# Softmax attention on one Trainium2 core: all four quarters of the value product directly behind the sums

## Chip, cores, metric

One NeuronCore of a Trainium2 chip runs the whole program. The metric is the device time of one execution in microseconds (us), taken as the median of several runs. The program has nine stages one after the other; the change touches only the softmax attention.

## What is computed

The program is a small network on x of shape (8, 512, 128): a quantised feed-forward layer, softmax attention, the feed-forward layer again, a mixture of experts, six layers of linear attention, the mixture again. The attention has 16 heads of 64, computed on the layer norm of x and added to x:

```python
q = split_heads(x @ Wq.T); k = split_heads(x @ Wk.T); v = split_heads(x @ Wv.T)
sim = jnp.einsum('bhid,bhjd->bhij', q, k) * scale
attn = safe_softmax(sim)
out = jnp.einsum('bhij,bhjd->bhid', attn, v)
return out.transpose(0, 2, 1, 3).reshape(B, N, INNER) @ Wo.T + bo
```

## The kernel before

The attention (attn_stage, L544 to L873) works on pairs of heads. A unit g is one pair of one batch, so there are 8 x 8 = 64 units (0 to 63), each with 512 queries and 512 keys. Every engine has its own hand-written loop over periods g = -2 to 66, and the engines meet through semaphores. In period g, TensorE (PE) works on several units at once: the scores of g+1, the transposed scores of g, the value product of g-1, the output product of g-3 and the projections of g+2. A period has four parts, kt = 0 to 3, one for each quarter of 128 keys (or of 128 queries):

- scores_turned(g, kt), L760 to L770: three pairs of fp16 products (high and low halves of q and k) write the transposed scores of a quarter of the keys into the banks turned[0] and turned[1], one for each head. The pair of one step runs on different row halves of the array. Each head's first product waits until ScalarE (ACT) has taken the exponential of the quarter before out of that head's bank (exp_done). less_maximum(g, kt), L772 to L778, is the fourth pair: it subtracts the row maxima, and its end lets ACT go (exp, L707 to L713).
- scores(g+1, qt), L742 to L750: a pair of fp16 products for a quarter of the queries of the next unit, written to score[0] and score[1]. It waits until VectorE (DVE) has reduced the quarter before (s_read). neg_max, L620 to L626, is that pair of DVE reductions. I call the products of part kt "turned kt" and "scores kt".
- project(g+2, 0) in part 0 and project(g+2, 1) in part 2, L780 to L799: the projections of q and of k, three fp16 products each. They go to the one bank proj. ACT copies the high half out (high, L694) and DVE then forms the low half (low, L636 to L642). project(g, 2) in part 3, L800 to L805, is the projection of v, twelve products into the same bank, and so it waits for low of k of unit g+2 (lo_done).
- max_turned(g+1), L752 to L758, at the end of part 3: one product that transposes the maxima. It waits for all eight reductions of unit g+1 (s_read at 8(g+2)). DVE turns its result into mdiag (max_rows, L628), which less_maximum of part 0 of the next period needs.
- add_up(g-1), L807 to L817, in part 1: the sums of the exponentials, from the tiles that GpSimd (POOL) adds up on L611. Behind it ACT (total_out), DVE (invert, L648) and eight SBUF copies on SyncE's queue (L596) prepare the reciprocals with which DVE normalises a period later (L655, o_done).
- values(g-1, kt), L819 to L828: a quarter of the value product, one fp32 product for each head (on different column halves of the array), accumulated in the bank pv over the four quarters. The first quarter waits for o_done of the unit before. The last quarter's end is pv_done, which lets ACT overwrite v and the exponentials two units on.
- output(g-3), L830 to L839: four fp32 products in part 0.

PE's order inside a period is only that of the code at L842 to L872. The value product stands in three places of it: quarters 0 and 1 in part 1, quarter 2 behind project(g+2, 1), quarter 3 in front of project(g, 2).

Of the kernel before, what the change touches and what calls it, by code (L numbers as in the profile page):

```python
# [18 lines left out]
TPB = 4  # L19
# [524 lines left out]
def attn_stage(nc, mem, tag):  # L544
# [5 lines left out]
    with ExitStack() as ctx:  # L550
# [29 lines left out]
        live = lambda g: 0 <= g < PAIRS_ALL  # L580
        PERIODS = range(-2, PAIRS_ALL + 3)

        with nc.Block() as block:
# [155 lines left out]
            def _(pe):  # L739
                XY = [(0, 0), (0, 1), (1, 0)]  # L740

                def scores(g, qt):  # L742
                    if qt == 0:
                        pe.wait_ge(hi_done, 2 * g + 2)
                    if g or qt:
                        pe.wait_ge(s_read, 8 * g + 2 * qt)
                    for head in range(2):
                        rows = halves[head]
                        nc.tensor.matmul(score[head][:], high_of[0][g % RING][rows, qt * P:(qt + 1) * P], high_of[1][g % RING][rows, :],  # L749
                                         start=True, stop=True).then_inc(s_done, 1)  # L750

                def max_turned(g):  # L752
                    pe.wait_ge(s_read, 8 * (g + 1))
                    if g:
                        pe.wait_ge(m_out, g)
                    if g >= 2:
                        pe.wait_ge(total_done, g - 1)
                    nc.tensor.transpose(max_bank, nmax[:], mem["ident"][:]).then_inc(m_done, 1)  # L758

                def scores_turned(g, kt):  # L760
                    k = g % RING
                    tile = slice(kt * P, (kt + 1) * P)
                    if kt == 0:
                        pe.wait_ge(lo_done, 2 * g + 2)
                    for n, (k_of, q_of) in enumerate(((high_of, high_of), (high_of, low_of), (low_of, high_of))):
                        for head in range(2):
                            if n == 0 and (g or kt):
                                pe.wait_ge(exp_done, 8 * g + 2 * kt + head - 1)
                            rows = halves[head]
                            nc.tensor.matmul(turned[head][:], k_of[1][k][rows, tile], q_of[0][k][rows, :], start=(n == 0), stop=False)  # L770

                def less_maximum(g, kt):  # L772
                    if kt == 0:
                        pe.wait_ge(m_out, g + 1)
                    for head in range(2):
                        rows = halves[head]
                        nc.tensor.matmul(turned[head][:], unit[rows, :], mdiag[rows, :, :].rearrange("p t q -> p (t q)"), start=False,  # L777
                                         stop=True).then_inc(t_done, 1)  # L778

                def project(g, which):  # L780
                    b, pair = divmod(g, PAIRS)
                    cols = slice(pair * P, (pair + 1) * P)
                    w = mem["w_attn16"][:, which]
                    x = lambda part_i, first, n: mem["xT"][:, part_i, b * SEQ + first:b * SEQ + first + n]
                    if which == 0:
                        if g >= 3:
                            pe.wait_ge(v_out, g - 2)
                        if g:
                            pe.wait_ge(lo_done, 2 * g)
                    elif which == 1:  # L790
                        pe.wait_ge(lo_done, 2 * g + 1)
                    else:
                        pe.wait_ge(lo_done, 2 * min(g + 3, PAIRS_ALL))
                        if g:
                            pe.wait_ge(v_out, g)
                    if which < 2:
                        for i, (w_part, x_part) in enumerate(XY):
                            last = nc.tensor.matmul(proj[:], w[:, w_part, cols], x(x_part, 0, SEQ), start=(i == 0), stop=(i == 2))  # L798
                        last.then_inc(qk_done, 1)  # L799
                    else:  # L800
                        for t in range(TPB):
                            for i, (x_part, w_part) in enumerate(XY):
                                last = nc.tensor.matmul(proj[:, t * P:(t + 1) * P], x(x_part, t * P, P), w[:, w_part, cols],
                                                        start=(i == 0), stop=(i == 2))
                        last.then_inc(v_done, 1)  # L805

                def add_up(g):  # L807
                    pe.wait_ge(added, 2 * (g + 1))
                    if g:
                        pe.wait_ge(total_done, g)  # L810
                    pe.wait_ge(m_out, min(g + 2, PAIRS_ALL))
                    for head in range(2):
                        for half in range(2):
                            first = (2 * head + half) * QUAD
                            last = nc.tensor.matmul(sums[first:first + QUAD, 0:HALF], ones[:],
                                                    psum[g % 2][:, head, half * HALF:(half + 1) * HALF], start=True, stop=True)
                    last.then_inc(sums_done, 1)  # L817

                def values(g, kt):  # L819
                    if kt == 0:  # L820
                        pe.wait_ge(v_out, g + 1)
                        if g:
                            pe.wait_ge(o_done, g)
                    for head in range(2):
                        last = nc.tensor.matmul(pv[halves[head], :], vv[g % 2][:, kt, halves[head]], pT[g % 2][:, head, kt, :],  # L825
                                                start=(kt == 0), stop=(kt == TPB - 1))
                    if kt == TPB - 1:
                        last.then_inc(pv_done, 1)  # L828

                def output(g):  # L830
                    pair = g % PAIRS
                    pe.wait_ge(o_done, g + 1)
                    if pair == 0 and g:
                        pe.wait_ge(x_added, g // PAIRS)
                    for t in range(TPB):
                        tile = slice(t * P, (t + 1) * P)
                        last = nc.tensor.matmul(out[:, tile], oT[g % 2][:, tile], mem["woT"][:, pair, :],
                                                start=(pair == 0 and t == 0), stop=(pair == PAIRS - 1), skip_group_check=True)
                    last.then_inc(out_done, 1)  # L839

                pe.wait_ge(set_up, 2)
                for g in PERIODS:  # L842
                    for kt in range(TPB):
                        if live(g):
                            scores_turned(g, kt)
                            if kt:
                                less_maximum(g, kt)
                        if live(g + 1):
                            scores(g + 1, kt)
                        if kt == 0:  # L850
                            if live(g):
                                less_maximum(g, 0)
                            if live(g + 2):
                                project(g + 2, 0)
                            if live(g - 3):
                                output(g - 3)
                        elif kt == 1 and live(g - 1):
                            add_up(g - 1)
                            values(g - 1, 0)
                            values(g - 1, 1)  # L860
                        elif kt == 2:
                            if live(g + 2):
                                project(g + 2, 1)
                            if live(g - 1):
                                values(g - 1, 2)
                        elif kt == 3:
                            if live(g - 1):
                                values(g - 1, 3)
                            if live(g):
                                project(g, 2)  # L870
                            if live(g + 1):
                                max_turned(g + 1)  # L872
# [765 lines left out]
```

## Time and profile before

| | |
|---|---|
| median of 3 runs | 2076.28 us (2074.09 to 2078.01) |
| profiled execution | 2078.86 us, span 2077.1 us |
| PE, DVE, ACT, POOL busy over the span | 74%, 71%, 42%, 49% |
| attention (first to last product on PE) | about 254 to 1071 us |
| PE, DVE, ACT, POOL busy between 400 and 600 us | 200.00, 152.27, 99.33, 122.60 us |
| granted PE clock between 400 and 600 us | 1.00 |

The span is the time from the first to the last recorded instruction; the execution's own time is 1.8 us longer. Matmul records overlap (the next one starts before the modelled end of the one before), so the time that a group of products takes on PE is read from the start of the group to the start of what follows it, not from its busy time.

### The profile page before, as it was taken

To read this page: it belongs to the slowest core of one execution; us is meant where nothing else is said; L and a number is where in the kernel's file an instruction comes from. 1 tells how busy PE (TensorE), PEld (TensorE's weight loads), DVE (VectorE), ACT (ScalarE), POOL (GpSimd) and SP (SyncE) were. 2 spreads that over 40 slices of the span, in tenths; PEclk is the share of its full clock that TensorE was granted. 3 is DMA by queue.
4 is the path that set the end of the run, shared out by engine and by line. 5 is a ranking of instruction groups with operands and counts; after the bars stand their busy time and mean duration, and the time that the engine had idled before them with its cause. 6 is when DMAs were issued, how large, how long until landed. Compare 5 with 4: busy or idle time off the path is not lost. (4 is left out here: it accounts for less than half of the span.)

```text
span 2077.1 us, 32008 instructions
## 1 busy us (share of the span) xinstructions
PE 1545.9 (74%) x10355; PEld 871.5 (42%) x10355; DVE 1483.7 (71%) x3141; ACT 865.7 (42%) x2102; POOL 1021.2 (49%) x1332
## 2 busy tenths in 40 slices
PE   0556389999999999999965554249748888761596
PEld 0334233334333333333323444227437767651373
DVE  4888677777777777777758887438567777773484
ACT  0111345444544445454422222037336667630372
POOL 0111346666565666565632222747435555627473
PEclk9889689999999999999986886569879999975698
DMA  6000000000000000000000000223400000002235
GB/s 199 0 0 1 1 11 23 23 23 22 21 21 22 24 23 22 22 21 21 24 19 0 1 0 6 72 70 108 126 1 1 1 1 1 1 11 72 75 109 156
DMA packets 90179, 70.51 MB, mean 34 GB/s; under 512 B 16608, under 2 KB 84640, under 8 KB 90016
## 3 DMA queue, kind: packets, MB, share of 16 engines
q1 hardware_dynamic: 75776, 44.05, 7.9%
q0 software_dynamic: 8704, 18.89, 2.7%
q10 hardware_dynamic: 5536, 5.52, 0.9%
q8 instruction: 87, 1.43, 0.3%
q14 instruction: 76, 0.62, 0.1%
HBM read 29.32 MB, written 22.30 MB: 25 GB/s over the span
## 5 line engine op out<-in xcount | busy, mean ns | idle before, releaser
L625 DVE TENSOR_REDUCE at_nmax<-at_score 128x1 f32<-128x512 f32 x512 | 329.9, 686 | 143.3 <-PE at_score L749 143.3
L713 ACT ACTIVATE at_pT<-at_turned 128x512 f32<-128x512 f32 x512 | 277.9, 595 | 342.8 <-PE at_turned L777 342.8
L611 POOL TENSOR_TENSOR m_rows<-m_rows,at_pT 128x512 f32<-128x512 f32 x256 | 319.5, 1269 | 95.0 <-ACT at_pT L713 95.0
L611 POOL TENSOR_TENSOR m_rows<-at_pT 128x512 f32<-128x512 f32 x128 | 160.2, 1271 | 227.6 <-ACT at_pT L713 227.6
L825 PE MATMUL at_pv<-at_pT,at_v 128*64 128x512 f32 x1024 | 261.7, 611 | 0.3 <-DVE at_oT L655 0.3
L1016 POOL DMA_INDIRECT by_token<-m_ysb,m_dest x144 | 137.9, 957 | 88.3 <-DVE m_ysb L1096 54.1
L1010 POOL DMA_INDIRECT by_expert<-m_rows,m_slot x128 | 123.5, 965 | 73.5 <-issue 38.4
L419 PE MATMUL f_gate<-m_wguT,f_xqT 128*128 128x352 f32 x128 | 63.3, 583 | 104.2 <-DVEq L337 102.8
L365 POOL TENSOR_TENSOR f_hq<-f_hg,f_hsc 128x704 f32<-128x704 f32 x32 | 44.3, 1384 | 195.2 <-DVEq L341 195.2
L115 DVE TENSOR_SCALAR la_xn<-la_y,la_ln_mean,la_ln_rstd 128x128 f32<-128x128 f32 x192 | 81.5, 485 | 53.6 <-POOLq L1438 53.6
L381 ACT ACTIVATE f_silu<-f_gate 128x704 f32<-128x704 f32 x32 | 24.2, 757 | 220.5 <-PE f_up L420 220.5
L648 DVE RECIPROCAL m_rows<-m_rows 128x256 f32<-128x256 f32 x64 | 111.6, 1743 | 2.9 <-ACT m_rows L719 2.9
L798 PE MATMUL at_proj<-m_rows 128*128 128x512 f16 x384 | 108.4, 392 | 5.3 <-DVE at_own L669 3.6
L1267 PE MATMUL m_h<-m_w,m_x 128*128 x432 | 109.8, 392 | 3.0 <-DVE m_x L1073 3.0
L1256 PE MATMUL m_x<-m_ident,m_xin 128*128 128x128 f32 x144 | 23.8, 292 | 112.8 <-DMA m_xin<-by_expert 112.8
L825 PEld LDWEIGHTS at_pv<-at_pT,at_v 128*64 128x64 f32 x1024 | 56.8, 135 | 117.6 <-issue 117.6
L770 PE MATMUL at_turned<-at_high_q,at_high_k 64*128 64x512 f16 x512 | 102.2, 388 | 0.8 <-ACT at_pT L713 0.5
L749 PE MATMUL at_score<-at_high_k,at_high_q 64*128 64x512 f16 x512 | 99.3, 381 | 2.8 <-DVE at_nmax L625 2.1
L770 PE MATMUL at_turned<-at_low_q,at_high_k 64*128 64x512 f16 x512 | 98.9, 378 | 0.0
L777 PE MATMUL at_turned<-at_mdiag,at_unit 64*128 64x512 f16 x512 | 98.8, 378 | 0.0
L770 PE MATMUL at_turned<-at_high_q,at_low_k 64*128 64x512 f16 x512 | 98.8, 377 | 0.0
L1500 PE MATMUL la_th<-m_ident,la_xn 128*128 128x128 f32 x192 | 33.8, 302 | 70.2 <-DVE la_xn L115 68.2
(311 smaller groups left out, 3665.4 us busy)
## 6 DMA issues: line engine op xcount, KB each, us to landing
m_rows<-m_rows SPq DMA_DIRECT2D x512, 32.0 KB, 1.8
m_xin<-by_expert SPq DMA_DIRECT2D x144, 72.0 KB
m_rows<-by_token SPq DMA_DIRECT2D x32, 256.0 KB, 4.8
by_token<-m_ysb,m_dest POOLq DMA_INDIRECT x144, 2.4
m_x<-in_x SPq DMA_DIRECT2D x8, 256.0 KB, 4.9
by_expert<-m_rows,m_slot POOLq DMA_INDIRECT x128, 2.3
out_x<-m_x SPq DMA_DIRECT2D x8, 256.0 KB, 3.9
by_expert<-m_pad SPq DMA_DIRECT2D x18, 72.0 KB, 1.6
```

The source lines that it names most:

```text
L611: done = nc.gpsimd.tensor_tensor(acc, before, pT[g % 2][:, head, kt, :], ALU.add)
L625: nc.vector.tensor_reduce(nmax[:, head * DH + qt:head * DH + qt + 1], score[head][:], AX.X, ALU.max, negate=True)\
L648: nc.vector.reciprocal(packed, total).then_inc(packed_done, 1)
L713: nc.scalar.activation(pT[g % 2][:, head, kt, :], turned[head][:], ACT.Exp).then_inc(exp_done, 1)
L749: nc.tensor.matmul(score[head][:], high_of[0][g % RING][rows, qt * P:(qt + 1) * P], high_of[1][g % RING][rows, :], start=True, stop=True). ...
L770: nc.tensor.matmul(turned[head][:], k_of[1][k][rows, tile], q_of[0][k][rows, :], start=(n == 0), stop=False)
L777: nc.tensor.matmul(turned[head][:], unit[rows, :], mdiag[rows, :, :].rearrange("p t q -> p (t q)"), start=False, stop=True).then_inc(t_don ...
L798: last = nc.tensor.matmul(proj[:], w[:, w_part, cols], x(x_part, 0, SEQ), start=(i == 0), stop=(i == 2))
L825: last = nc.tensor.matmul(pv[halves[head], :], vv[g % 2][:, kt, halves[head]], pT[g % 2][:, head, kt, :], start=(kt == 0), stop=(kt == TPB ...
L1010: nc.gpsimd.indirect_dma_start(dram_rows, bass.IndirectOffsetOnAxis(slot[:, k, t:t + 1], 0), rows[k][:, t, :], None).then_inc(scattered, 16)
L1016: nc.gpsimd.indirect_dma_start(mem["dram_y_all"], bass.IndirectOffsetOnAxis(dest[j // TPB % DESTS][:, j % TPB:j % TPB + 1], 0), ysb[q % YS ...
L1267: last = nc.tensor.matmul(h[j % 3][:], x16[n % 2][:, x_part, tile], mem["w12_16"][:, w_part, ds(e, 1), :].rearrange("p e h -> p (e h)"), s ...
```

## The change

PE's order inside a period changes. The quarters 2 and 3 of the value product, which stood behind the projection of k and in front of the projection of v, now follow quarters 0 and 1 directly in part 1. No instruction is added or removed, on any engine, and no wait is edited.

```diff
@@ -856,16 +856,11 @@
                                 output(g - 3)
                         elif kt == 1 and live(g - 1):
                             add_up(g - 1)
-                            values(g - 1, 0)
-                            values(g - 1, 1)
-                        elif kt == 2:
-                            if live(g + 2):
-                                project(g + 2, 1)
-                            if live(g - 1):
-                                values(g - 1, 2)
+                            for part in range(TPB):
+                                values(g - 1, part)
+                        elif kt == 2 and live(g + 2):
+                            project(g + 2, 1)
                         elif kt == 3:
-                            if live(g - 1):
-                                values(g - 1, 3)
                             if live(g):
                                 project(g, 2)
                             if live(g + 1):
```

PE's order from the sums in part 1 to turned 3, before (at_turned are the transposed scores, at_score the scores, at_proj a projection, at_pv the value product; L770 and L777 are the four pairs of scores_turned and less_maximum):

```order
L815 MATMUL at_sums<-m_rows 32x256 x4
L825 MATMUL at_pv<-at_pT,at_v 64x512 x4
L770 MATMUL at_turned<-at_high_q,at_high_k 128x512 x2
L770 MATMUL at_turned<-at_low_q,at_high_k 128x512 x2
L770 MATMUL at_turned<-at_high_q,at_low_k 128x512 x2
L777 MATMUL at_turned<-at_mdiag,at_unit 128x512 x2
L749 MATMUL at_score<-at_high_k,at_high_q 128x512 x2
L798 MATMUL at_proj<-m_rows 128x512 x3
L825 MATMUL at_pv<-at_pT,at_v 64x512 x2
```

The same place now:

```order
L815 MATMUL at_sums<-m_rows 32x256 x4
L825 MATMUL at_pv<-at_pT,at_v 64x512 x8
L770 MATMUL at_turned<-at_high_q,at_high_k 128x512 x2
L770 MATMUL at_turned<-at_low_q,at_high_k 128x512 x2
L770 MATMUL at_turned<-at_high_q,at_low_k 128x512 x2
L777 MATMUL at_turned<-at_mdiag,at_unit 128x512 x2
L749 MATMUL at_score<-at_high_k,at_high_q 128x512 x2
L798 MATMUL at_proj<-m_rows 128x512 x3
L770 MATMUL at_turned<-at_high_q,at_high_k 128x512 x2
```

Eight value products stand behind the sums where four stood, and turned 3 follows the projection of k directly.

PE's order from scores 3 to the next period, before, with the semaphores that each product waits for:

```order
L749 MATMUL at_score<-at_high_k,at_high_q 128x512 [waits at_s_read]
L749 MATMUL at_score<-at_high_k,at_high_q 128x512
L825 MATMUL at_pv<-at_pT,at_v 64x512 x2
L803 MATMUL at_proj<-m_rows 128x128 [waits at_v_out,at_lo_done]
L803 MATMUL at_proj<-m_rows 128x128 x11
L758 MATMUL at_sums<-m_ident,at_nmax 128x128 [waits at_total_done,at_m_out,at_s_read]
L770 MATMUL at_turned<-at_high_q,at_high_k 128x512 [waits at_exp_done,at_lo_done]
```

The same place now:

```order
L749 MATMUL at_score<-at_high_k,at_high_q 128x512 [waits at_s_read]
L749 MATMUL at_score<-at_high_k,at_high_q 128x512
L803 MATMUL at_proj<-m_rows 128x128 [waits at_v_out,at_lo_done]
L803 MATMUL at_proj<-m_rows 128x128 x11
L758 MATMUL at_sums<-m_ident,at_nmax 128x128 [waits at_total_done,at_m_out,at_s_read]
L770 MATMUL at_turned<-at_high_q,at_high_k 128x512 [waits at_exp_done,at_lo_done]
```

Between scores 3 and the transposition of the maxima only the projection of v is left.

## Rows read from the trace of the kernel before

**Rows 1.** Groups of instructions, PE, 281 to 1043 us: count | busy us, mean ns | idle before.

```profile
L825 PE MATMUL at_pv<-at_pT,at_v 128*64 128x512 f32 x976 | 249.9, 612 | 0.0
L758 PE MATMUL at_sums<-m_ident,at_nmax 128*128 128x128 f32 x61 | 17.0, 278 | 0.0
```

**Rows 2.** Line L758, all its instructions: duration ns min/median/max, first and last start.

```profile
L758 PE MATMUL at_sums<-m_ident,at_nmax x64: 277/278/474, 268.8 to 1052.3; 128*128 128x128 f32 x64
```

**Rows 3.** Timeline of a steady period: start us, duration us, engine, line [idle before].

```profile
608.59 1.94 PE L825 MATMUL at_pv<-at_pT,at_v 128*64 128x512 f32 x8
...
610.46 0.39 PE L770 MATMUL at_turned<-at_high_q,at_high_k 64*128 64x512 f16 x2
...
611.34 0.38 PE L749 MATMUL at_score<-at_high_k,at_high_q 64*128 64x512 f16 x2
611.53 1.09 ACT L713 ACTIVATE at_pT<-at_turned 128x512 f32<-128x512 f32 x2 [2.26 <-PE at_turned L777]
611.65 0.82 PE L798 MATMUL at_proj<-m_rows 128*128 128x512 f16 x3
611.75 1.29 DVE L625 TENSOR_REDUCE at_nmax<-at_score 128x1 f32<-128x512 f32 x2 [0.67 <-PE at_score L749]
...
612.40 1.08 PE L825 MATMUL at_pv<-at_pT,at_v 128*64 128x512 f32 x4
612.51 0.60 ACT L699 ACTIVATE at_high_k<-at_proj 128x512 f16<-128x512 f32 x1
613.14 0.69 DVE L641 SCALAR_TENSOR_TENSOR at_low_k<-at_proj,at_high_k 128x512 f16<-128x512 f32 x1
613.41 0.39 PE L770 MATMUL at_turned<-at_high_q,at_high_k 64*128 64x512 f16 x2
...
614.70 1.29 DVE L625 TENSOR_REDUCE at_nmax<-at_score 128x1 f32<-128x512 f32 x2 [0.87 <-PE at_score L749]
615.15 2.50 POOL L611 TENSOR_TENSOR m_rows<-m_rows,at_pT 128x512 f32<-128x512 f32 x2 [0.46 <-ACT at_pT L713]
...
616.28 0.28 PE L758 MATMUL at_sums<-m_ident,at_nmax 128*128 128x128 f32 x1
...
616.50 0.39 PE L770 MATMUL at_turned<-at_high_q,at_high_k 64*128 64x512 f16 x2
```

**Rows 4.** Timeline at the end of the attention, PE.

```profile
1065.12 0.64 PE L815 MATMUL at_sums<-m_rows 128*32 128x256 f32 x8 [0.77 <-POOL m_rows L611]
...
1066.09 3.65 PE L825 MATMUL at_pv<-at_pT,at_v 128*64 128x512 f32 x16 [0.34 <-DVE at_oT L655]
...
1069.68 1.16 PE L837 MATMUL at_out<-m_woT,at_oT 128*128 128x128 f32 x8
```

**Rows 5.** Timeline of period 1, from the exponentials of part 0 on.

```profile
281.37 1.08 ACT L713 ACTIVATE at_pT<-at_turned 128x512 f32<-128x512 f32 x2 [1.27 <-PE at_turned L777]
...
282.52 0.60 PE L770 MATMUL at_turned<-at_low_q,at_high_k 64*128 64x512 f16 x2
...
283.18 0.59 PE L749 MATMUL at_score<-at_high_k,at_high_q 64*128 64x512 f16 x2
```

**Rows 6.** Timeline of period 0, which has no value product.

```profile
270.08 0.64 PE L770 MATMUL at_turned<-at_high_q,at_low_k 64*128 64x512 f16 x2
...
275.21 0.60 PE L770 MATMUL at_turned<-at_low_q,at_high_k 64*128 64x512 f16 x2
...
277.88 0.69 DVE L641 SCALAR_TENSOR_TENSOR at_low_k<-at_proj,at_high_k 128x512 f16<-128x512 f32 x1 [0.28 <-ACT at_high_k L699]
...
278.49 1.28 DVE L625 TENSOR_REDUCE at_nmax<-at_score 128x1 f32<-128x512 f32 x2
278.63 0.84 PE L803 MATMUL at_proj<-m_rows 128*128 128x128 f16 x12 [0.17 <-DVE at_low_k L641]
...
279.82 0.33 PE L758 MATMUL at_sums<-m_ident,at_nmax 128*128 128x128 f32 x1 [0.35 <-DVE at_nmax L625]
280.08 0.39 PE L770 MATMUL at_turned<-at_high_q,at_high_k 64*128 64x512 f16 x2
```

**Rows 7.** Windows: us, busy PE, PEld, DVE, ACT, POOL, granted clock, DMA share, GB/s.

```profile
280.00:290.00 10.00, 9.90 (x67) 2.99 (x66) 7.55 (x10) 4.67 (x10) 6.76 (x6) 1.00 0.06 15
```

## The prediction

> **What bounds the kernel now.** I read the groups of PE's instructions over the attention first, to see whether PE waits at all. Between 281 and 1043 us it doesn't: the 976 value products and the 61 transpositions of the maxima have 0.0 us of idle time before them [rows 1]. So PE's own order of products is the bound there, and each period costs what its products cost. The line of the transposition gives the period: its last start is at 1052.3, that of unit 1 at 279.82 [rows 2, 6], 62 periods later, so a period is (1052.3 - 279.8) / 62 = 12.46 us.
>
> Then I read the timeline of one period, to see which of PE's waits are nearly due, because an order that starts a product earlier runs into them [rows 3]. I call the start of turned 2 X (610.46). The next period's turned 0 starts at 616.50, X + 6.04. In between, the reader should see two answers that PE needs back. The exponentials of turned 2 end at 611.53 + 1.09 = X + 2.16, and turned 3 starts at X + 2.95: 0.8 us of slack, and quarter 2 of the value product (612.40 to 613.41, 1.01 us) fills it. The reductions of scores 3 end at 614.70 + 1.29 = 615.99, and the transposition of the maxima starts at 616.28: 0.29 us of slack, and quarter 3 stands in front of it too. The two quarters that the change takes away are the cover of these two round trips.
>
> **The change, part by part.**
>
> *Four quarters in one block.* Quarters 0 and 1 take 610.46 - 608.59 = 1.87 us [rows 3]. The block of four is in the trace too, behind the last period: 1069.68 - 1066.09 = 3.59 us [rows 4]. Everything behind the block in part 1 moves back by 3.59 - 1.87 = **+1.72 us**. Nothing in the block waits anew: the exponentials of unit g-1 were all read by the sums in front of it, and o_done, on which the first quarter waits, belongs to a chain (sums, reciprocal, eight copies, normalise) of which the change moves nothing, in a period that gets no shorter.
>
> *Turned 3 comes up to the exponentials.* The projection of k still starts at X + 1.19 and would free PE at about X + 1.94 (612.40 is its end now). Turned 3 of the second head has to wait for the second exponential, at X + 2.16. How PE goes on behind such a wait is shown by period 1: exponentials end at 281.37 + 1.08 = 282.45, the second pair of products starts at 282.52, 0.07 later, and the scores at 283.18, another 0.66 later [rows 5]. So the second pair starts at X + 2.23 and scores 3 at X + 2.89.
>
> *The projection of v.* It needs the low half of k. The high half starts at 612.51 = X + 2.05 and the low half at 613.14 = X + 2.68, and ends at X + 3.37; both hang on the exponentials and the projection of k, which don't move against X. In period 0 the projection of v started 0.06 us after that end (278.57 to 278.63) [rows 6]: X + 3.43. A wait of a few hundredths, hidden by the next.
>
> *The transposition of the maxima.* DVE starts the reductions 0.41 us after the scores (611.34 to 611.75) [rows 3], so those of scores 3 at X + 2.89 + 0.41 = X + 3.30, if the low half of k lets them: it ends at X + 3.37, and operations on DVE start up to 0.08 before the end of the last (278.49 against 278.57) [rows 6]. I take X + 3.32. They end at X + 4.61, and the transposition starts 0.05 later, as in period 0 (279.77 to 279.82): X + 4.66. The next turned 0 follows 0.22 (616.28 to 616.50) to 0.26 us later (279.82 to 280.08): **X + 4.90**. Parts 2 and 3 thus give back 6.04 - 4.90 = 1.14 us of the 2.02 us that stood there in value products.
>
> *Sum.* A period gets longer by 1.72 - 1.14 = +0.58 us. Periods 1 to 61 are whole: 61 x 0.58 = +35.4. Period 62 has no projection of k: it was shorter before by that product's 0.75 us (611.65 to 612.40), but the round trips stay, so +1.3. In period 63 POOL ends the wait for the last sums already now (0.77 us idle, rows 4), and its additions follow exponentials that come 1.7 us later: +1.8. Total **+38.5 us**. The profiled execution took 2078.86 us (span 2077.1, the rest of the stages unchanged), which gives 2117.4; it lay 2.6 us above the median of the runs, 2076.28, so I forecast 2115 for the median.
>
> *What costs nothing, and its cover.* POOL: its additions of part 3 now end at 617.65 = X + 7.19; two additions take 2.50 us and those of part 2 begin about 1.8 us behind X, so they will end by X + 6.8, and the next value block begins at 608.59 + 12.46 = X + 10.6 before and X + 9.5 after. About 2 us are left. ACT has the v copy and the exponentials of part 0 behind the same events as in period 0. Turned 0 follows exponentials of part 3 that end at about X + 4.2. pv_done comes earlier, and so nobody waits longer for it. SyncE and POOL issue the same DMAs in the same order.
>
> **Bounds.** A whole stretch with this order and these waits, PE, ACT and DVE together, is period 0, which has no value product. There turned 2 starts in two halves, since it is itself held by exponentials; counted from its second pair (275.21 less the 0.23 of a pair) X is 274.98, and turned 0 starts at 280.08: X + 5.10 [rows 6]. That is +0.78 per period, +50.7 in all, 2127. I take X + 4.90 because in a steady period turned 2 follows the value block and starts whole, so the scores and the projection of k are about 0.2 us earlier against the exponentials. The lower end of this case would be scores 3 not held by the exponentials, with only the low half and its reductions in the way: that saves under 0.1 per period, 2109.
>
> **Rivals.**
>
> *Fewer switches win, waits do not show (faster).* A quarter alone costs 1.01 us (612.40 to 613.41), a further quarter in the block 0.86 (half of 1.72), so PE saves 0.15 twice in a period: 0.30 x 63 = 19 us, **2057**. It decides if the two waits together take less than 0.30 us in a period. For it speaks that PE has been the only bound; against it, that the second wait has 0.29 us of slack and loses 1.01 us of cover, and that period 0 shows 0.35 us of idle time at that very product. The Trainium skill, page TensorEngine Tiling (Array Packing), section Key Properties, says that changing the tiling mode drains TensorE; by that rule the change is a gain, and the trace agrees with the rule but the rule does not see the waits.
>
> *The waits just eat the saving (no change).* Same place, with the two waits near 0.30: 2076. It needs PE to be held 0.6 us less than period 0 shows.
>
> *The whole of period 0's stretch (slower by more).* 2122 to 2130, if the steady period is held like period 0.
>
> *The clock falls.* With about half a microsecond of idle time in each period, PE's granted clock might drop to the lower level (1.2 GHz). In the first products of period 0, before the clock had risen, a pair took 0.64 us against 0.38 later [rows 6, 3]; five such pairs in each period are 5 x 0.26 x 62 = 81 us more: about **2195**. Against it: the window behind period 0's gap shows a granted clock of 1.00 [rows 7]. The Trainium skill, page TensorE: Matmul & The Clock Gate, Part 1, says that idleness of PE brings the throttle back; by that rule this rival has a cause, and no row here shows a fall behind so short a gap.
>
> **How the numbers follow.** The chain above has 0.78, forecast 2115. Period 0's whole stretch has 0.10, the clock 0.03, the faster rival 0.05, no change 0.04. The range 2104 to 2130 takes in the first two with their bounds and leaves out the others and a little of the edges. A measurement of this kernel can tell about 0.2% (4 us) from no change. Faster by more than that 0.05, within 0.04, slower 0.91.
>
> **What would show it.** In the timeline after, a steady period of about 13.04 us between transpositions. The value products as one row of sixteen records, 3.59 us to turned 2. Turned 2 to the next turned 0 in 4.9 us. In the groups, about 0.4 us of idle time before each transposition on L758 (it starts at X + 4.66, the records of the v projection end 0.84 after X + 3.43), released by the reductions on L625, 61 times, some 24 us; turned 3 split in two halves, as in period 1. A granted clock of 1.00. Wrong would be: a period under 12.46; no idle time before L758; idle time at the value block, with o_done or the sums as releaser; or a clock under 1.

## The result and the profile after

| | before | after |
|---|---|---|
| median | 2075.19 us | 2115.07 us |
| profiled execution, span | 2078.86, 2077.1 us | 2115.31, 2113.6 us |
| ratio of the times | | 1.0188, 95% interval 1.0168 to 1.0208 |
| period (start to start of L758, unit 1 to the last, by 62) | 12.459 us | 13.075 us |
| the first 61 of these 62 alone | 12.476 us | 13.080 us |
| the last of them (period 62, no projection of k) | 11.42 us | 12.77 us |

The change makes the kernel slower by 1.9%. The forecast was 2115, in a range of 2104 to 2130. Single executions far above the rest (3341.5 us here, one of four) are left out of the ratios, and without it the median is 2114.82 us.

The groups of PE's instructions during the attention (281 to 1080 us), the same two as in [rows 1]:

```profile
L825 PE MATMUL at_pv<-at_pT,at_v 128*64 128x512 f32 x976 | 222.9, 599 | 0.0
...
L758 PE MATMUL at_sums<-m_ident,at_nmax 128*128 128x128 f32 x61 | 20.0, 328 | 23.9 <-DVE at_nmax L625 23.9
```

The value products still wait for nothing. The transposition of the maxima, which had no idle time before it, now has 23.9 us, 0.39 us each time, and the releaser is the DVE reduction L625. The idle column shows less than PE loses, since a record's modelled end lies behind the point at which the next product could start.

A steady period of the kernel after, as its timeline shows it; it answers to [rows 3], and X is now 626.29:

```profile
622.70 3.65 PE L825 MATMUL at_pv<-at_pT,at_v 128*64 128x512 f32 x16
...
626.29 0.39 PE L770 MATMUL at_turned<-at_high_q,at_high_k 64*128 64x512 f16 x2
...
627.36 1.08 ACT L713 ACTIVATE at_pT<-at_turned 128x512 f32<-128x512 f32 x2 [3.98 <-PE at_turned L777]
627.48 0.82 PE L798 MATMUL at_proj<-m_rows 128*128 128x512 f16 x3
...
628.23 0.66 PE L770 MATMUL at_turned<-at_high_q,at_high_k 64*128 64x512 f16 x2
628.33 0.60 ACT L699 ACTIVATE at_high_k<-at_proj 128x512 f16<-128x512 f32 x1
628.50 0.60 PE L770 MATMUL at_turned<-at_low_q,at_high_k 64*128 64x512 f16 x2
...
628.97 0.69 DVE L641 SCALAR_TENSOR_TENSOR at_low_k<-at_proj,at_high_k 128x512 f16<-128x512 f32 x1
629.16 0.59 PE L749 MATMUL at_score<-at_high_k,at_high_q 64*128 64x512 f16 x2
...
629.61 1.29 DVE L625 TENSOR_REDUCE at_nmax<-at_score 128x1 f32<-128x512 f32 x2
629.72 0.84 PE L803 MATMUL at_proj<-m_rows 128*128 128x128 f16 x12
...
630.95 0.33 PE L758 MATMUL at_sums<-m_ident,at_nmax 128*128 128x128 f32 x1 [0.39 <-DVE at_nmax L625]
631.22 0.39 PE L770 MATMUL at_turned<-at_high_q,at_high_k 64*128 64x512 f16 x2
...
632.40 0.82 PE L798 MATMUL at_proj<-m_rows 128*128 128x512 f16 x3
...
633.06 1.05 PE L837 MATMUL at_out<-m_woT,at_oT 128*128 128x128 f32 x8
```

Three things are to be seen. The block takes 626.29 - 622.70 = 3.59 us. Turned 3 (628.23) is recorded with 0.66 us instead of 0.39 and its following pairs with 0.60 and 0.59 instead of 0.38: the two heads no longer run in step, because the second head waited for the second exponential (627.36 + 1.08 = 628.44). And from the end of the projection of v (629.72 + 0.68 = 630.40) to 630.95 PE has nothing to do; 0.68 us is what that projection takes in the kernel before (615.60 to 616.28). Turned 2 to the next turned 0 takes 4.93 us instead of 6.04.

The reductions of scores 3 (629.61) follow the low half of k on DVE without a gap, and that ends at 628.97 + 0.69 = 629.66. The scores alone would have let them start at 629.16 + 0.41 = 629.57. So even with a turned 3 that isn't held, the low half of k would have kept the reductions about where they are. No run has that case alone.

The end of the attention, which answers to [rows 4]:

```profile
1103.46 0.64 PE L815 MATMUL at_sums<-m_rows 128*32 128x256 f32 x8 [1.77 <-POOL m_rows L611]
1104.03 5.35 PE L825 MATMUL at_pv<-at_pT,at_v 128*64 128x512 f32 x16
...
1109.31 1.16 PE L837 MATMUL at_out<-m_woT,at_oT 128*128 128x128 f32 x8
...
1113.36 1.16 PE L837 MATMUL at_out<-m_woT,at_oT 128*128 128x128 f32 x8 [2.89 <-DVE at_oT L655]
```

POOL's wait is 1.77 us instead of 0.77, and from the last transposition (1088.84; before 1052.25) to the last output product (1113.36; before 1075.03) it takes 24.52 us instead of 22.78. (The last output product before is thus at 1075.03 us; the attention ends there, and not at the 1071 us of the table of the kernel before.)

The account of the profiled executions closes: 62 periods x 0.616 = +38.2, the end +1.7, everything in front of them -1.6 (the transposition of unit 1 starts at 278.21 instead of 279.82), the stages behind it -1.8: +36.5, which is the difference of the spans. The -1.6 and the -1.8 lie in instructions that the change leaves as they were, and profiles differ there by more than that: from the last output product to the end of the span it takes 997.2 us in e9 and 1005.0 us in e4.

### The profile page after: what moved, and what is told of

Its sections match the earlier page's. It is cut to its first block and busy times, and to the rows that moved or that the text cites. A ratio compares the mean times of both kernels' runs of the same rounds, so it can differ in the third digit from the quotient of the medians.

```text
span 2113.6 us, 32008 instructions
## 1 busy us (share of the span) xinstructions
PE 1561.0 (74%) x10355; PEld 892.1 (42%) x10355; DVE 1479.8 (70%) x3141; ACT 865.3 (41%) x2102; POOL 1018.5 (48%) x1332
## 5 line engine op out<-in xcount | busy, mean ns | idle before, releaser
L625 DVE TENSOR_REDUCE at_nmax<-at_score 128x1 f32<-128x512 f32 x512 | 329.8, 686 | 196.7 <-PE at_score L749 196.7
L825 PE MATMUL at_pv<-at_pT,at_v 128*64 128x512 f32 x1024 | 235.5, 602 | 0.0
L825 PEld LDWEIGHTS at_pv<-at_pT,at_v 128*64 128x64 f32 x1024 | 68.2, 137 | 137.3 <-issue 137.3
L770 PE MATMUL at_turned<-at_high_q,at_high_k 64*128 64x512 f16 x512 | 118.9, 388 | 2.1 <-ACT at_pT L713 1.6
L749 PE MATMUL at_score<-at_high_k,at_high_q 64*128 64x512 f16 x512 | 112.2, 381 | 2.8 <-DVE at_nmax L625 2.1
L770 PE MATMUL at_turned<-at_low_q,at_high_k 64*128 64x512 f16 x512 | 112.4, 378 | 0.0
L777 PE MATMUL at_turned<-at_mdiag,at_unit 64*128 64x512 f16 x512 | 111.7, 377 | 0.0
L770 PE MATMUL at_turned<-at_high_q,at_low_k 64*128 64x512 f16 x512 | 111.7, 377 | 0.0
```

The costliest lines, as they stand in the source:

```text
L625: nc.vector.tensor_reduce(nmax[:, head * DH + qt:head * DH + qt + 1], score[head][:], AX.X, ALU.max, negate=True)\
```

## The experiments

The theory: PE has two round trips in parts 2 and 3 (turned 2 over ACT to turned 3; scores 3 over DVE to the transposition), a value quarter was the cover of each, and the time lost is what they lack in cover, less 0.15 us for each place of value products saved. The main rival: the long block in part 1 costs by its length, because it keeps turned 2, and so ACT, DVE and POOL, waiting. Periods below are read as in the table above: the start of L758 of unit 1 to that of the last unit, divided by 62.

**e1: quarter 3 stays.** Against the kernel before:

```diff
                                 values(g - 1, 0)
                                 values(g - 1, 1)
+                                values(g - 1, 2)
...
                                 project(g + 2, 1)
-                            if live(g - 1):
-                                values(g - 1, 2)
```

> Quarters 0 to 2 in part 1, none in part 2, quarter 3 back in front of the projection of v. Cover theory (the two round trips cost, each by its own cover): the block adds 0.86 us; turned 3 is still held by the exponentials (scores 3 at X + 2.89, quarter 3 from X + 3.40 to 4.41, projection of v to 5.09, by which time the reductions have ended at 4.61), so the next turned 0 starts at X + 5.30 instead of X + 6.04. Net +0.12 us a period, about +8 us: 2083, and no idle time before L758. Rival (the long block in part 1 is what costs, in proportion to the quarters moved into it): half of the change, about +20 us, 2095.

Measured: 2085.74 us, ratio 1.0043 (1.0028 to 1.0058), +9 us; the period is 12.588, +0.13. Its timeline behind turned 2 (625.05):

```profile
627.92 0.59 PE L749 MATMUL at_score<-at_high_k,at_high_q 64*128 64x512 f16 x2
...
628.36 1.29 DVE L625 TENSOR_REDUCE at_nmax<-at_score 128x1 f32<-128x512 f32 x2
628.44 1.08 PE L825 MATMUL at_pv<-at_pT,at_v 128*64 128x512 f32 x4
629.45 0.84 PE L803 MATMUL at_proj<-m_rows 128*128 128x128 f16 x12
630.13 0.28 PE L758 MATMUL at_sums<-m_ident,at_nmax 128*128 128x128 f32 x1
630.34 0.39 PE L770 MATMUL at_turned<-at_high_q,at_high_k 64*128 64x512 f16 x2
```

The reductions end at 629.65, before the projection of v does, so L758 waits for nothing; turned 0 starts at X + 5.29 (forecast X + 5.30). Only the first trip is short of cover.

**e2: quarter 2's place stays, quarter 3 is in it.** Against the kernel before:

```diff
                                 values(g - 1, 0)
                                 values(g - 1, 1)
+                                values(g - 1, 2)
...
                             if live(g - 1):
-                                values(g - 1, 2)
-                        elif kt == 3:
-                            if live(g - 1):
                                 values(g - 1, 3)
+                        elif kt == 3:
```

> Quarters 0 to 2 in part 1, quarter 3 in part 2 where quarter 2 was, none in part 3. Cover theory: turned 3 starts at X + 2.95 as before, scores 3 at X + 3.83, their reductions run from X + 4.24 to 5.53, the transposition at X + 5.58, turned 0 at X + 5.82 instead of 6.04: -0.22 + 0.86 = +0.64 us a period, about +42 us: 2117, as slow as the whole change although one quarter less moved into part 1, with some 0.7 us of idle time before each L758. Rival (block length in part 1): as e1, 2095.

Measured: 2119.77 us, ratio 1.0207 (1.0187 to 1.0228), +43 us; the period is 13.123, +0.66. Part 3 in its timeline:

```profile
633.52 0.84 PE L803 MATMUL at_proj<-m_rows 128*128 128x128 f16 x12
633.62 1.29 DVE L625 TENSOR_REDUCE at_nmax<-at_score 128x1 f32<-128x512 f32 x2 [0.86 <-PE at_score L749]
...
634.97 0.33 PE L758 MATMUL at_sums<-m_ident,at_nmax 128*128 128x128 f32 x1 [0.60 <-DVE at_nmax L625]
```

e1 and e2 have the same block of three in part 1, and one costs five times the other. That settles it against the block's length. It also shows that the place with no cover in part 3 is the dear one, and that filling part 2 alone buys nothing.

**e3: the second trip made short.** The changed kernel with

```diff
-                        nc.vector.tensor_reduce(nmax[:, head * DH + qt:head * DH + qt + 1], score[head][:], AX.X, ALU.max, negate=True)\
+                        seen = score[head][:, 0:P] if qt == 3 else score[head][:]
+                        nc.vector.tensor_reduce(nmax[:, head * DH + qt:head * DH + qt + 1], seen, AX.X, ALU.max, negate=True)\
```

> The changed kernel, but the DVE reductions of scores 3 look at 128 of 512 columns (the row maximum of that quarter of the queries is taken over a quarter of the keys). Cover theory: the reductions end at about X + 3.9, before the projection of v does (X + 4.11), so nothing waits at L758 and the next turned 0 starts at X + 4.32 to 4.37: 0 to +0.05 us a period against the kernel before, 2076 to 2080. Rival (block length, or starved ACT and POOL): stays near 2115.

Measured: 2076.79 us, ratio 1.0007 (0.9997 to 1.0017); the period is 12.469, +0.01. Its timeline:

```profile
624.29 0.49 DVE L626 TENSOR_REDUCE at_nmax<-at_score 128x1 f32<-128x128 f32 x2
624.40 0.84 PE L804 MATMUL at_proj<-m_rows 128*128 128x128 f16 x12
625.08 0.28 PE L759 MATMUL at_sums<-m_ident,at_nmax 128*128 128x128 f32 x1
```

With the order of the change untouched and its block still 3.59 us long, 0.8 us less on DVE takes the whole loss away. Turned 3 is still held as in the change (scores 3 start at X + 2.87), so the first trip still costs, and the two places saved pay for it.

**e4: all the trips made short.** e3, and the same cut, to 128 of 512 columns, for the exponentials of part 2 and the low half of k. The rest of both is left stale, so this kernel no longer computes the attention; it is run for its time alone.

```diff
-                        nc.scalar.activation(pT[g % 2][:, head, kt, :], turned[head][:], ACT.Exp).then_inc(exp_done, 1)
+                        part = slice(0, P if g >= 2 and kt == 2 else SEQ)
+                        nc.scalar.activation(pT[g % 2][:, head, kt, part], turned[head][:, part], ACT.Exp).then_inc(exp_done, 1)
...
+                    part = slice(0, P if g >= RING and which else SEQ)
+                    nc.vector.scalar_tensor_tensor(out=low_of[which][g % RING][:, part], in0=proj[:, part], scalar=scale,
...
```

> e3, and in addition the exponentials of part 2 (from unit 2 on) and the low half of k (from unit 3 on) are taken of 128 of 512 columns only, the rest is left stale. Cover theory: turned 3 starts whole at X + 1.94, the projection of v at X + 3.13, the transposition at X + 3.85, turned 0 at X + 4.07: 1.72 - 1.97 = -0.25 us a period, about -15 us: 2060. That would show the 0.30 us that the change saves in switches, which the waits hide. Rival (no switch is saved): 2076 or above.

Measured: 2065.68 us, ratio 0.9945 (0.9925 to 0.9964), -11 us; the period is 12.295, -0.16 where -0.25 was expected. The block does save time on PE, and the waits hide it. The difference is mainly a trip that I had left out: with part 3 so short, turned 0 comes up to the exponentials of part 3.

```profile
621.05 1.09 ACT L717 ACTIVATE at_pT<-at_turned 128x512 f32<-128x512 f32 x2 [0.37 <-PE at_turned L781]
...
622.08 0.51 PE L774 MATMUL at_turned<-at_high_q,at_high_k 64*128 64x512 f16 x2
```

0.51 us instead of 0.39 in turned 0: the second head is 0.12 late, and stays so through all its products. (Parts 2 and 3 themselves came out 0.03 shorter than expected: turned 2 starts at 618.04, turned 0 at X + 4.04.)

The Trainium skill, page TensorEngine Tiling (Array Packing), section Key Properties, says that a change of tiling mode drains TensorE. The rows are in line with it: a quarter alone costs 1.01 us, one more in a block 0.86, and no more than that 0.15 us is to be had for a place. They also speak for the shape and against the number format as the cause of such costs. In the changed kernel the projection of q takes 0.66 us (632.40 to 633.06) in front of output products that are fp32 but on the whole array, and that of k takes 0.75 us (627.48 to 628.23) in front of fp16 products on row halves. What the 0.15 us behind a value block is made of, no run separates.

**e5: one, one and two.** The kernel before with quarter 0 in part 1, 1 in part 2, 2 and 3 in part 3:

```diff
                                 values(g - 1, 0)
-                            values(g - 1, 1)
...
-                                values(g - 1, 2)
+                                values(g - 1, 1)
...
                             if live(g - 1):
+                                values(g - 1, 2)
                                 values(g - 1, 3)
```

> The kernel before, but quarter 0 alone in part 1, quarter 1 in part 2, quarters 2 and 3 together in part 3: still three places. Cover theory: the part 1 trip (exponentials back 2.16 us behind turned 1, turned 2 now at 3.6) has room for 0.86 us less, the others keep or gain cover, the number of blocks is the same: no change, 2074 to 2079. Rival (an early value product is what matters, since pv_done lets ACT go): slower or faster by the 0.86 us that one quarter moved in each period, up to 53 us.

Measured: 2076.37 us, ratio 1.0003 (0.9992 to 1.0015); the period is 12.459, the same to the thousandth. A quarter moved between two places that both keep their cover costs nothing.

**e6: none, two and two.** Against the kernel before:

```diff
                             add_up(g - 1)
-                            values(g - 1, 0)
-                            values(g - 1, 1)
...
-                                values(g - 1, 2)
+                                values(g - 1, 0)
+                                values(g - 1, 1)
...
                             if live(g - 1):
+                                values(g - 1, 2)
                                 values(g - 1, 3)
```

> No quarter in part 1, two in part 2, two in part 3: one place less than before (saves 0.15 us a period), but turned 2 now follows the sums after 0.57 us and is held by the exponentials of part 1 (second pair 2.23 us behind the start of turned 1, scores 2 at 2.89, projection of k at 3.40 instead of 2.94). Cover theory: +0.46 - 0.15 = +0.31 us a period, about +19 us, 2095, no idle time before L758. Rival (fewer places is all that counts where the transposition is covered): -9 us, 2067.

Measured: 2094.28 us, ratio 1.0084 (1.0069 to 1.0099), +17 us; the period is 12.751, +0.29 where +0.31 was expected. The trip of part 1 has to be covered like the others: turned 2 is now the one in two halves.

```profile
626.67 1.08 ACT L713 ACTIVATE at_pT<-at_turned 128x512 f32<-128x512 f32 x2 [0.96 <-PE at_turned L777]
...
627.36 0.84 PE L770 MATMUL at_turned<-at_high_q,at_high_k 64*128 64x512 f16 x2
...
627.82 0.60 PE L770 MATMUL at_turned<-at_low_q,at_high_k 64*128 64x512 f16 x2
```

627.82 is 0.07 behind the end of the second exponential (627.75), as in [rows 5].

**e7: e6 with the projection of v as the cover of part 1.** Besides the move, its waits change to the new order of the bank proj, and ACT copies v in front of the exponentials of part 2:

```diff
                             if live(g - 1):
                                 add_up(g - 1)
+                            if live(g):
+                                project(g, 2)
...
-                            if live(g):
-                                project(g, 2)
                             if live(g + 1):
                                 max_turned(g + 1)
```

> As e6, and the projection of v (0.68 us) moves from part 3 into part 1, behind the sums, with ACT's copy of v in front of the exponentials of part 2. Cover theory: the projection is the cover that e6 lacks, turned 2 starts about 2.4 us behind turned 1 and is not held; part 3 keeps two quarters in front of the transposition. One place of value products less than before: -0.05 to -0.15 us a period, -3 to -9 us, 2067 to 2073, faster than both kernels. Rival (some other chain, such as ACT's order or the reductions behind the reciprocal on DVE, binds as soon as part 1 is short): 2080 or more, as e6.

Measured: 2074.26 us, ratio 0.9985 (0.9976 to 0.9993), -3 us. No product is held any more, and the 17 us of e6 are gone. But the saving of a place isn't in the period: 12.451, -0.01 where -0.05 to -0.15 was expected. It was given back twice, as its timeline shows:

```profile
632.49 0.84 PE L805 MATMUL at_proj<-m_rows 128*128 128x128 f16 x12
...
633.27 0.39 PE L770 MATMUL at_turned<-at_high_q,at_high_k 64*128 64x512 f16 x2
```

```profile
627.64 0.33 PE L758 MATMUL at_sums<-m_ident,at_nmax 128*128 128x128 f32 x1
627.90 0.39 PE L770 MATMUL at_turned<-at_high_q,at_high_k 64*128 64x512 f16 x2
```

The projection of v takes 0.78 us in front of products on row halves instead of 0.68 in front of the transposition (a change of shape once more, 0.10), and the transposition behind value products takes 0.26 instead of 0.22. The rest of the 3 us lies outside the periods, and I don't claim it for the order.

**e8: one block of four in part 3, with cover in part 2.** Against e7:

```diff
                                 project(g + 2, 1)
-                            if live(g - 1):
-                                values(g - 1, 0)
-                                values(g - 1, 1)
+                            if live(g - 3):
+                                output(g - 3, 1)
...
+                                values(g - 1, 0)
+                                values(g - 1, 1)
                                 values(g - 1, 2)
...
-                    for t in range(TPB):
+                    for t in range(2 * half, 2 * half + 2):
```

> From e7: all four quarters of the value product in one block in part 3, and the place in part 2 that they leave is covered by half of the output product (two of its four products, moved there from part 0; the addition to x on DVE moves to the end of the period). Cover theory, from the timeline of e7: part 0 gets 0.43 us shorter (turned 1 was 0.37 us behind the exponentials and its second pair 0.2 more, so it is just not held), part 2 gets 1.08 + 0.14 us instead of 0.75 + 1.87 us, part 3 3.58 instead of 1.86 us; no pair of turned is held, and the reductions of scores 3 end far ahead of L758. Period 12.36 us against 12.46, -0.10 us x 62 = -6 us: 2070, ratio 0.997. Rival (the block saves nothing by itself, the gain of e7 was chance): 2074 to 2077. Rival (a new hold behind the shortened part 0): period 12.5 or more, 2080 or more, with turned 1 in two halves.

Measured: 2074.17 us, ratio 0.9985 (0.9976 to 0.9995); the period is 12.441, -0.02 where -0.10 was expected. The second rival is half right: turned 1 is held, by the second head's 0.12 us.

```profile
628.10 0.51 PE L770 MATMUL at_turned<-at_high_q,at_high_k 64*128 64x512 f16 x2
```

**e9: the output product split three and one.** Against e8:

```diff
-                    for t in range(2 * half, 2 * half + 2):
+                    for t in ((0, 1, 2), (3,))[half]:
```

> e8 with three products of the output in part 0 and one in part 2. In e8 turned 1 was held by 0.12 us a period (its second head starts 0.07 behind the second exponential, and the lag stays through the ten products). With 0.21 us more in part 0 turned 1 should start 0.1 us behind that point and whole, and turned 3 about at the point itself (X + 2.19 against 2.23 for the second head, at most 0.04 of a lag). Cover theory: period 12.44 - 0.12 + 0.04 = 12.36 us, 2069 to 2070, ratio 0.997. Rival (the block's saving is given back by some other cost in any order): as e8, 2074.

Measured: 2068.15 us, ratio 0.9977 (0.9967 to 0.9986), -5 us; the period is 12.370, -0.09 against the kernel before. Both trips now have just their cover:

```profile
628.82 0.39 PE L770 MATMUL at_turned<-at_high_q,at_high_k 64*128 64x512 f16 x2
...
633.51 0.44 PE L770 MATMUL at_turned<-at_high_q,at_high_k 64*128 64x512 f16 x2
...
634.74 3.65 PE L827 MATMUL at_pv<-at_pT,at_v 128*64 128x512 f32 x16
638.33 0.33 PE L758 MATMUL at_sums<-m_ident,at_nmax 128*128 128x128 f32 x1
```

Turned 1 starts whole (0.39), turned 3 with a lag of 0.05 (0.44), and the four quarters stand in one block of 3.59 us. This is the change's aim, one place for the value product, in a version that beats both kernels: the change, without the cover, costs 0.62 x 62 = 38 us; the same block of four, with it, gains 0.09 x 62 = 5.5 us.

## Why the prediction was right

- *PE's order is the bound, and two trips are nearly due.* Right. All the time lost lies at turned 3, at L758 and between them.
- *The block.* 3.59 us, as forecast from the end of the attention. Nothing in it waits (0.0).
- *Turned 3.* Second pair at X + 2.21 (forecast 2.23), scores 3 at X + 2.87 (2.89).
- *Projection of v.* X + 3.43 (3.43).
- *Transposition.* Reductions at X + 3.32 (3.32), L758 at X + 4.66 (4.66), turned 0 at X + 4.93 (4.90).
- *Sum.* The mean of 62 periods grew by 0.616 us, but that mean takes in period 62, which the forecast counted by itself. Each of the other 61 grew by 0.604 (12.476 to 13.080; forecast 0.58), period 62 by 1.35 (forecast 1.3). The missing 0.02 is the step from L758 to turned 0: I took 0.24, between the two values that the trace had, and it was 0.26 in the median of the periods. I can't say why it is the longer one. PE stood still in front of L758 here, but in e7 the step is 0.26 too, and there value products stand directly in front. The end cost 1.7 against 1.8.
- *Idle time.* 23.9 us before L758, 61 times, against "some 24".
- *Why period 0's stretch (X + 5.10) was the wrong price.* The steady turned 2 does start whole (0.39 at 626.29), as argued, and turned 0 follows at X + 4.93.
- *The rivals.* "Fewer switches win" had the saving right (e4 shows more than half of the 0.30 us even with one trip still short) and its condition wrong. The clock stayed at 1.00 in the periods. Two prices there were misread. For the clock I compared durations, 0.64 and 0.38 us, which overlap from one pair to the next; from start to start a pair takes 0.43 us at 1.2 GHz (269.65 to 270.08 in period 0) and 0.22 at 2.4 GHz, so the five pairs come to 65 us and not 81. And "no change" needed PE to be held 0.78 us less than period 0 shows (5.10 against 4.32), and not 0.6, which is the distance from my own chain. Neither entered the forecast.

What the prediction did not say is which of the two trips is dear. e1 and e2 show it. Each saves one place (0.15 us). Net of that, the first trip alone costs 0.13 a period (e1), the second alone 0.66 (e2). Without the saving these are 0.28 and 0.81, and both together cost 0.92 in the change (0.62 and two places), less than their sum.

## What to carry to other kernels

On an engine that runs in order and is never idle, a product may look free to move, but it can be the cover of an answer that another engine still owes. Before moving it, write down for each wait of the engine how long the answer takes and how much work stands in front of it; moves that leave every answer its cover cost nothing (e5), and the cover may be any work (e7), down to a single product (e9). A gain in changes of shape is worth about 0.15 us a place here, and is soon lost: count the changes over the whole period, not only at the product that is moved.

## What was not expected of the hardware

A pair of products on the two row halves didn't catch up in these runs. Where only the second head's first product was late, by 0.12 us, all ten products behind it ran with that lag (e4, e8), and what followed them on the whole array was 0.11 to 0.12 us late: in e8 the sums start 1.30 us behind turned 1 (628.10 to 629.40) instead of 1.18. A wait of the second half was thus as dear as a wait of the whole.

And PE's clock, which I had feared for in the periods, did fall at the end of the attention. The windows there:

```profile
1090.00:1100.00 10.00, 9.21 (x60) 3.44 (x61) 2.24 (x2) 3.74 (x8) 4.91 (x5) 1.00 0.07 19
1100.00:1104.00 4.00, 2.23 (x28) 1.65 (x27) 0.69 (x1) 1.37 (x3) 3.40 (x3) 1.00 0.09 23
1104.00:1110.00 6.00, 6.00 (x26) 2.15 (x23) 1.75 (x1) 0.38 (x1) 0.00 (x0) 0.72 0.08 22
```

The mean of 0.72 in the last one is a stretch at 1.2 GHz and one at 2.4 GHz. In front of it PE had been idle for 0.69 and 1.77 us within the last periods' thin work, and the last block takes 1109.31 - 1104.03 = 5.28 us instead of the 3.59 us of [rows 4]. It cost nothing here: the last output product waits another 2.89 us for DVE, and from the sums to that product it takes 9.90 us (1103.46 to 1113.36), as it did before (1065.12 to 1075.03, 9.91), when the clock was 1.00 through the block. The 0.55 us of each steady period left the clock at 1.00. What between the two decides, no run here tells.
